# Twenty-three more unread matmuls per batch element in a decoder layer on one core

## The reference, cut to what matters

```
xs  = conv(x);  xs = xs + xs @ pe_w.T
q, k, v = split(xs @ qkv_w.T)                         # 16 heads of 16, as bf16
x1  = layernorm(x + softmax(q k' / 4) v @ out_w.T)
y   = softmax(causal(x1 Wq (x1 Wk)' / 4)) x1 Wv       # self, 16 heads
y  += softmax(x1 Wcq (ctx Wck)' / 4) ctx Wcv          # cross, 16 heads, 1024 columns
x2  = layernorm(x1 + y @ Wp + bp)
cluster, tile = argmax of gates(x2 @ signatures')     # 8 clusters of 8 tiles
h   = tanh(gelu(x2 @ cw1 + cb1) @ cw2 + cb2)
out = layernorm(layernorm(x2 + spline(h, params[tile]) * directions[tile]))
```

## Time and profile before

| | |
|---|---|
| median of 3 runs | 2343.53 us (2342.00 to 2348.82) |
| the profiled execution's own time | 2342.77 us |
| its span in the profile | 2341.0 us |
| mean granted TensorE clock | 0.962 of full speed |
| TensorE matmuls busy | 2178.3 us, 93% |
| VectorE busy | 1868.9 us, 80% |
| ScalarE busy | 1381.7 us, 59% |
| `unit(0)` of batch elements 1 to 7 begins at | 402.78, 682.58, 963.36, 1239.81, 1518.31, 1797.66, 2075.74 us |

### The profile page before, as it was taken

The page is one execution under the profiler, slowest core; times in us unless marked ns, Lnnn a source line. Parts: engine busy times, 40 slices in busy tenths (PEclk is TensorE's granted clock), DMA queues, the critical chain, the costliest instruction groups (busy, mean ns, idle before and its releaser), DMA issues.

```text
span 2341.0 us, 37315 instructions
## 1 busy us (share of the span) xinstructions
PE 2178.3 (93%) x12942; PEld 991.6 (42%) x12965; DVE 1868.9 (80%) x5137; ACT 1381.7 (59%) x2977; POOL 189.0 (8%) x349
## 2 busy tenths in 40 slices
PE   5999999999989999899999999999998999979992
PEld 2354434543345433454335543454334543335432
DVE  6858869788888879788797887978878886878844
ACT  2834677456864568546784457745686456844650
POOL 3011001000011000110001100110001100001000
PEclk7899999999999999999999999999999999999995
DMA  3600034000420005100160002400043000510000
GB/s 111 125 10 1 1 63 82 10 1 1 100 54 10 1 19 110 26 10 1 32 123 10 2 1 58 96 10 1 1 87 58 10 1 10 106 30 1 1 10 9
DMA packets 250844, 81.67 MB, mean 35 GB/s; under 512 B 236064, under 2 KB 247328, under 8 KB 250656
## 3 DMA queue, kind: packets, MB, share of 16 engines
q1 hardware_dynamic: 250656, 79.29, 16.6%
HBM read 16.35 MB, written 4.19 MB: 9 GB/s over the span
## 4 chain that ended last, share of the span: by engine, by line
PE 79%; DVE 9%; ACT 8%; issue 3%; DMA 1%; POOL 0%; SPq 0%; DVEq 0%; POOLq 0%; ACTq 0%
PE bank L1513 22%; PE bank L1566 13%; PE bank L1551 8%; PE bank L1204 6%; PE bank L1509 5%; PE bank L1470 4%; ACT work L603 4%; PE bank L1548 4%; PE bank L1333 3%; DVE work L770 3%; PE bank L1320 2%; PE bank L1526 2%; PE bank L1577 2%; PE bank L1356 1%; ACT work L659 1%
## 5 line engine op out<-in xcount | busy, mean ns | idle before, releaser
L659 ACT ACTIVATE work<-bank 128x512 f32<-128x512 f32 (+3 forms) x1536 | 737.8, 553 | 559.0 <-PE bank L1551 288.3
L1033 DVE TENSOR_REDUCE top_half<-bank 128x1 f32<-128x512 f32 x1024 | 625.3, 680 | 22.0 <-PE bank L1513 22.0
L1513 PE MATMUL bank<-k_c,q_c 32*128 32x512 f32 x2048 | 629.3, 635 | 0.0
L1551 PE MATMUL bank<-q_c,k_c 32*128 32x512 f32 x2048 | 548.9, 629 | 0.0
L603 ACT ACTIVATE work<-work,neg 128x512 bf16<-128x512 bf16 x512 | 362.7, 717 | 32.3 <-DVE work L770 32.3
L1513 PEld LDWEIGHTS bank<-k_c,q_c 32*128 32x128 f32 x2048 | 274.5, 184 | 244.6 <-DVE top_half L1033 159.4
L770 DVE TENSOR_SCALAR_CACHE_REDUCE work<-bank 128x512 bf16<-128x512 f32 x512 | 322.3, 686 | 46.4 <-PE bank L1302 32.5
L1566 PE MATMUL bank<-work,v_flat 128*32 128x512 f32 (+3 forms) x3072 | 320.9, 553 | 9.2 <-ACT work L659 8.8
L1030 DVE CUSTOM_DVE_ANT_0 masked<-bank,mask_w 128x384 bf16<-128x384 f32 (+3 forms) x512 | 223.8, 488 | 82.8 <-PE bank L1509 77.3
L1551 PEld LDWEIGHTS bank<-q_c,k_c 32*128 32x128 f32 x2048 | 227.0, 183 | 92.5 <-ACT work L659 57.2
L1548 PE MATMUL bank<-q_s,k_s 32*128 32x512 f32 (+3 forms) x1024 | 258.7, 473 | 0.0
(11 more groups left out here) (194 smaller groups left out, 2183.8 us busy)
## 6 DMA issues: line engine op xcount, KB each, us to landing
xT_pad<-xT SPq DMA_DIRECT2D x16, 256.0 KB, 3.3
ctx_sb<-ctxT SPq DMA_DIRECT2D x8, 512.0 KB, 3.3
x_res<-x SPq DMA_DIRECT2D x8, 512.0 KB, 4.7
out<-r_sb SPq DMA_DIRECT2D x8, 512.0 KB, 3.3
work<-work SPq DMA_TRANSPOSE x112, 4.4
qk_sb<-qkT SPq DMA_DIRECT2D x1, 512.0 KB, 4.6
pe_sb<-pe_w SPq DMA_DIRECT2D x1, 256.0 KB, 3.9
v_sb<-vT SPq DMA_DIRECT2D x1, 256.0 KB, 6.4
```

Source lines behind the costliest of these rows:

```text
L659: nc.scalar.activation(pT[:, s % PT_SLOTS, g, q0:S], exp_bank(n)[:, 0:S - q0], ACT.Exp, scale=SCALE).then_inc(pT_ready, 1)
L1033: nc.vector.tensor_reduce(top_half[:, i % 2, g, u // 2, u % 2:u % 2 + 1], scores, AX.X, ALU.max, negate=True).then_inc(slot_out, 1)
L1513: mm(dst, q_c[rows, i, P * t:P * (t + 1)], k_c[rows, i, S * half:S * (half + 1)], start=True, stop=True, tile_position=(GW * g, 0)).then_i ...
L1551: mm(dst, k_c[rows, i, P * u:P * (u + 1)], q_c[rows, i, :], start=True, stop=True, tile_position=(GW * g, 0)).then_inc(sT_mm, 1)
```

## The change

It adds calls of `keep_clock` at four places of the TensorE program, and two waits ahead of them. No other engine's instructions change.

- Site A, between `pv1(11)` and `pv1(12)`: a wait for all `s1_evac` of this batch element, then 8 unread matmuls into bank 3. In every batch element.
- Site B, ahead of the first score matmul of the lead: 4 into bank 6. In every batch element.
- Site C, ahead of `expert_columns`: 3 into bank 6. With `prev`, so in batch elements 1 to 7.
- Site D, behind `scores(4, ...)` and ahead of `unit(4)`: a wait for the eighth `pj_evac` of the batch element, by which the result of `unit(3)` has been copied out of bank 7, then 8 into bank 7. With `prev`.

```diff
                 pv1(H - 5)
+                pe.wait_ge(s1_evac, (b + 1) * H * NT)
+                keep_clock(3, FILLERS)
                 pv1(H - 4)
                 transpose_tiles(H - 2)
...
                     kind, i, u = part_of(m)
+                    if m == 0 and r == 0:
+                        keep_clock(6, FILLERS // 2)
                     if r == 0 and u == 0:
...
                     if prev and m == EXPERT_LEAD:
+                        keep_clock(6, FILLERS // 2 - 1)
                         expert_columns(c, base, uses)
+                    if prev and m == 4:
+                        pe.wait_ge(pj_evac, b * 2 * UNITS + 8)
+                        keep_clock(7, FILLERS)
                     if m in VALUES_LEAD:
```

## The result

| | before | changed |
|---|---|---|
| median, 5 runs each | 2344.26 us (2342.00 to 2356.20) | 2331.65 us (2327.66 to 2336.26) |
| time of the profiled execution | 2342.77 us | 2336.26 us |
| span, mean granted clock | 2341.0 us, 0.962 | 2334.5 us, 0.967 |

The ratio is 0.9935, with a 95% interval from 0.9907 to 0.9964: 0.65% faster, or 12.6 us between the medians. The forecast was 2337.0 us and 6.5 us less. Between the two *profiled* executions the difference is 6.5 us; the changed kernel's happened to be the slowest of its five.

The account below looks back on a forecast made before the run. TensorE, with 79% of the chain, was taken to bound the kernel. From 2342.8 us, less 5.2 us (clock at D) and 1.1 us (clock at A), plus 0.5 us (waits at A), came 2337.0 us, range 2331 to 2345 us.

Parts of the forecast that it names:

- Covers: Idle TensorE time covers the unread matmuls: cost 0 at sites B, C and D, 0.5 us at A.
- The clock at D: Seven stretches from the end of scores(4) to the first L1566 stay at full clock, saving 5.2 us.
- The sum: Whole kernel: 2342.8 - 5.2 (D) - 1.1 (A) + 0.5 (waits at A) = 2337.0 us.
- What the clock gives back: Clock falls prevented behind the sites: 5.2 us gained at D, 1.1 us at A, nothing from B and C.
- Sites B and C at zero: No clock fall directly follows the waits at sites B and C, so no gain was taken there.
- Site A was priced at 1.1 us: Clock falls behind site A, up to unit(0), in elements 0 and 4: 1.1 us gained, ends 0 and 1.9 us.
- rival 2: The clock fall isn't held, or comes elsewhere, as in the scores behind unit(4): 2340 to 2345 us, chance 0.24.
- Rival 1: More falls go: B and C also hold unit(3), faster leads carry through: 2328 to 2335 us, chance 0.16.
- Rival 3: At D and A unread matmuls run at the lower clock and become the wait: 2350 to 2358 us, chance 0.06.

Follow-up runs that it names:

- sixteen: Site D alone with 16 unread matmuls in place of 8, against the kernel before: median 2336.06 us, ratio 0.9980.
- e1_d: Only site D of the change kept, against the kernel before: median 2330.44 us over 5 runs, ratio 0.9949.
- e11_d: Only site D of the change kept, run again, against the kernel before: median 2331.75 us over 12 runs, ratio 0.9963.
- e2_a: Only site A of the change kept, against the kernel before: median 2340.88 us over 11 runs, ratio 0.9991.
- e5_wait: Only site D's wait for pj_evac kept, without its matmuls, against the kernel before: median 2341.45 us over 12 runs, ratio 0.9996.
- e4_ad: Only sites A and D of the change kept, against the kernel before: median 2335.70 us over 7 runs, ratio 0.9970.
- e7_shift: Site D alone plus 8 unread matmuls once in the lead of batch element 0, against the kernel before: median 2333.35 us, ratio 0.9956.
- b1: The kernel before, unchanged, profiled a second time: 2333.08 us.
- b3: The kernel before, unchanged, profiled a fourth time: 2331.09 us.
- b2: The kernel before, unchanged, profiled a third time: 2344.38 us.

## Why the prediction was right and wrong

- **Covers, right.** B, C and D cost nothing: in element 2 the starts of what is queued behind them did not move. `pv1(12)` was 0.2 us late there, as forecast (0.16 us), and `pv1(13)` only 0.04 us; alone site A is 0.1% faster, if anything.
- **The clock at D, right in kind.** The seven stretches are at 1.00 and sum to 176.8 us. The term was 5.2 us; profile against profile it measures 6.0 us, on average over 17 profiles 4.2 us. The wait of 0.38 us for VectorE behind `unit(4)` is there as forecast, and it is part of why sixteen cost only 0.4 us an element.
- **The sum, wrong by its size.** The failed step is the term for site D in "What the clock gives back", 5.2 us: it priced a fall at D by the length of its own stretch up to the first L1566 and held the rest as it was. Site D alone measured 12.7 us between medians in e1_d and 8.8 us in e11_d; over all executions it is 10.0 us (mean of 17: 2332.2 us) and the change 9.1 us (mean of 17: 2333.1 us) under the kernel before. The term's own part was right, even a little high, at 4.2 us; what is missing lies outside the seven stretches. There the rest did not stay as it was: in the profiles the main loops of elements 1 to 6 became about 2 us shorter in all, the last one 1.3 us longer. In executions, low time went down by 182 - 144 = 38 us. Over the 87 of the kernel before a least-squares line gives 0.32 us for each us of low time, 12 us for 38: more than what came off, and far from the 0.18 us for which 5.2 us in 28 us stands. The 12.6 us of the result are in part luck of the draw: over all executions the change brings 9.1 us, 0.39%, against the 6.5 us that were forecast.
- **Sites B and C at zero, right** within 0.1%, which the interval, 0.22% faster to level, hardly tells from nothing. Site A was priced at 1.1 us; e2_a lies 1.0 us (means) to 2.3 us (medians) under the kernel before.
- **The Trainium skill's rule.** The section "HAM oscillation — how this bites in real kernels" on the page "TensorE: Matmul & The Clock Gate" of the Trainium skill lays the fall of the clock to waits longer than that of site D. In these traces the clock fell in that wait of 1.8 us or up to 1.2 us behind it (42 of the 45 falls at D in the nine profiles without unread matmuls), and it hardly did once the wait was filled (2 of 56 elements), but did with the wait for `pj_evac` alone (e5_wait). In e4_ad it fell with no idle time ahead. Here the measurement decides against the rule as a complete one, and rival 2 falls in the form that it has there: the fall at D was held. Its other half, that a fall comes elsewhere, is what the last element shows.
- **Rival 1** named the right direction, more than the rows at D say, with a chance of 0.16, though not through B and C. Rival 3's mechanism exists, in one element each of e4_ad and e7_shift, far too seldom to turn the sign. Its 2355 us is 2342.8 + 12; the 5 us named beside it are not taken off.

Three things stay open. The nine profiled executions without site D have a mean of 2338.1 us, 4 us under the mean of the 87, and between them and the six with it the spans differ by only 3.6 us, of which 4.5 us are in elements 1 to 7 and 0.9 us the other way ahead of them. So more than half of the 10 us is seen in no profile, and where it comes off isn't shown. That a fall at D brings the later ones on was not shown apart from both following from how an execution lies in time. And whether the same matmuls somewhere else between `unit(3)` and `unit(4)`, not in the wait, would have held the clock as well was not tried.

## What to carry to other kernels

The worth of a filled wait isn't what the stretch behind it shows, if the clock falls elsewhere too: falls further on can go with it, or come in its place. Price it by the time and the granted clock of whole executions, over several, and not by the one that was profiled. Find the wait behind which the clock falls in most rounds of the loop and fill that one first, to just under its length; here the others in the loop added nothing that could be measured. Work that is never read is free only as long as the wait lasts, and costs double if the clock is low when it starts (3.39 us in place of 1.74 us in e4_ad).

## What the hardware showed that was not expected

- The falls recur at the same places: e4_ad and e7_shift, two programs, had the same falls from element 1 on but for one, b1 and b3 from element 1 on. In the last element the first fall stood at 23 to 24 us in nine profiles of nine, and with site D at 58 us in six of six.
- One execution of the kernel before took 2331.09 us and another 2356.20 us, with nothing changed. The time of the 87 goes with their low time at 0.32 us per us.
- The clock can fall, and stay at the lower level, through dense work: in e4_ad it fell in `gather` with TensorE busy all the time, and in b2 it stayed low for 17 us, over `unit(3)`, `gather` and `unit(4)`, in which TensorE was 15.5 us busy.
